# First expert matrix loaded from HBM for each slot instead of copied on the chip from a resident set

## The chip, the cores and the metric

The kernel runs on one core of one Trainium2 chip. The metric is the time of one execution on the device in microseconds (us). Three runs of the kernel before took 895.51, 890.18 and 890.01 us; their median is 890.18 us.

## What is computed

One decoder layer in float32 on x of shape (4, 512, 256): self-attention, cross-attention to a context of 64 rows for each batch, and a mixture of 8 experts with the best 2 for each token, with a layer norm after each. The part that the change touches is the last:

```python
logits = einsum('bsd,ed->bse', x, router_w)          # 8 experts
topk_vals, topk_idx = top_k(softmax(logits), 2)      # for each of 2048 tokens
out = zeros_like(x_flat)                             # 2048 x 256
for eid in range(8):
    w = sum(where(idx == eid, vals, 0), axis=-1)
    h = gelu(x_flat @ w1[eid].T, approximate=False)  # w1[e]: 1024 x 256, 1 MB in float32
    y = h @ w2[eid].T                                # w2[e]: 256 x 1024, 1 MB in float32
    out = out + w[:, None] * y
```

The result is layernorm(x + out).

## The kernel before, in words

The attention stages come first and are not touched. During the second of them and after it SyncE (SP) loads the weights of the experts into `wexp`, one `load_expert(e)` for each expert (lines 462 to 468): two DMAs of 1 MB, w1 and then w2, which wait until the expert before has landed. Experts 0 to 5 are loaded in and just behind the cross-attention, expert 6 when the input of the expert stage has been stored (line 481), and expert 7 between the loads of the meta rows (line 496).

The router decides on the chip which tokens go to which expert. GpSimd (POOL) scatters token numbers and weights into the table `metas` in HBM (line 664, 32 indirect DMAs of 128 rows). VectorE (DVE) makes two plans of 39 entries (`NSLOT` = 39 slots of 128 tokens): `plan[0]` names the expert of each slot, `plan[1]` the row in `metas` where its tokens begin. It signals `s_planned`.

Then the expert stage runs over the 39 slots:

- SP waits for the plan and for all scatters to have landed (lines 484 to 486). For each slot t it reads `plan[1]` into a register and issues a 1 KB DMA from `metas` to `mt` (`load_meta`, lines 488 to 490). The slots form three groups, 0 to 3, 4 to 7 and 8 to 38, written out one behind another, with `load_expert(7)` behind the first group. After this SP has nothing to do until the last sums are stored (line 499).
- POOL gathers the 128 rows of slot t from `x2d` (line 695), three slots ahead of the scatter; later it adds the weighted output of the slot to `acc` (line 703), one slot at a time.
- VectorE and ScalarE (ACT) copy the w1 of the slot's expert from `wexp` to one of two buffers `w1c`, a half each (`copy_w1`, line 361), when slot t-2 has been through its first matmuls (`s_mm1`).
- TensorE (PE) works in order (`tile`, line 1597): `hidden(t+1)` (32 matmuls of w1 and the turned tokens, line 1582), `turn_tile(t+2)` (2 transposes, line 1570), `expert_out(t)` (16 matmuls with w2, line 1593). `hidden(t)` waits for both halves of `w1c` and for the turned tokens.
- ACT copies the turned tokens (line 845) and does the gelu (line 851); DVE weighs the output (line 1209).

Ahead of the loop PE does `turn_tile(0)`, `hidden(0)`, `turn_tile(1)`. All waits of an engine hold up what stands behind them in that engine's list, and SP's list is one such list.

Of the kernel before, what the change touches and what calls it, by code (L numbers as in the profile page):

```python
# [18 lines left out]
ACT = mybir.ActivationFunctionType  # L19
AX = mybir.AxisListType  # L20

P = 128
NB, S, D = 4, 512, 256
# [5 lines left out]
KD = D // P  # L29
NE, FF = 8, 1024  # L30
KF = FF // P
# [14 lines left out]
NSLOT = (2 * T) // P + NE - 1  # L46
# [5 lines left out]
def decoder_layer(nc, x, xT, ctxT, wqT, wkT, wvT, woT, xwq, xbq, xwk, xbk, xwv, xbv, xwo, xbo,  # L52
# [16 lines left out]
    def sb(name, cols, dt, region, rows=P):  # L69

        width = cols * (2 if dt == BF16 else 4)
        at = place.get(region, region)
        place[region] = at + (width + 31) // 32 * 32
        return nc.alloc_sbuf_tensor_at(name, [rows, cols], dt, offset=at)

    def sem(name):
        return ctx.enter_context(nc.semaphore(name))

    def ds(start, n):
        return slice(start, start + n) if isinstance(start, int) else bass.ds(start, n)  # L80
# [39 lines left out]
    plan = [sb(f"plan{i}", NSLOT, I32, R_CONST, 1) for i in range(2)]  # L120
# [69 lines left out]
    rstd = sb("rstd", QT, F32, Y_REG)  # L190
    assert place[Y_REG] <= R_K + 64 * KB

    EW = KD * FF + KF * D
    place[R_Q] = R_Q
    wexp = sb("wexp", NE * EW, F32, R_Q)

    place[R_O] = R_O
    w1c = [sb(f"w1c{i}", KD * FF, F32, R_O) for i in range(2)]
# [77 lines left out]
    s_planned = sem("plan_ready")  # L276
    s_we = sem("expert_weights_loaded")
# [4 lines left out]
    s_xtT = sem("tile_x_copied")  # L282
    s_mm1 = sem("hidden_ready")
    s_h = sem("gelu_ready")
    s_w1c = [sem(f"w1_copied_{k}") for k in range(KD)]
    s_mm2 = sem("expert_out_ready")
    s_yw = sem("weighted_out_ready")
    s_sc = sem("outputs_added")
# [64 lines left out]
    def max2_rows(queue, b):  # L353
        queue.wait_ge(s_m2c, b + 1)
        for hh in range(2):
            for r in range(3):
                queue.dma_start(qst[ROWS + r:ROWS + r + 1, ds(b * H * S + hh * H * S // 2, H * S // 2)]
                             .rearrange("p (a t) -> p a t", t=P),
                             mT2[8 * QT * r:8 * QT * (r + 1), hh * P:(hh + 1) * P]).then_inc(s_m2l, 16)

    def copy_w1(engine, copy, t, j, k):

        e = engine.value_load(plan[0][0:1, ds(t, 1)], min_val=0, max_val=NE - 1)
        engine.wait_ge(s_we, 32 * (e + 1))
        if not (isinstance(t, int) and t < 2):
            engine.wait_ge(s_mm1, t - 1)
        copy(w1c[j % 2][:, k * FF:(k + 1) * FF], wexp[:, ds(e * EW + k * FF, FF)]).then_inc(s_w1c[k], 1)  # L367

    def third_part(engine, b, qk):
        p_v = parts[qk][:, :].rearrange("p (m r t) -> p m r t", m=KD, r=3)  # L370
# [4 lines left out]
    def _(sp):  # L375
# [85 lines left out]

        def load_expert(e):
            if e > 0:
                sp.wait_ge(s_we, 32 * e)
            sp.dma_start(wexp[:, ds(e * EW, KD * FF)].rearrange("p (k f) -> p k f", k=KD),
                         w1T[ds(e, 1)].rearrange("e (k p) f -> p (e k) f", p=P)).then_inc(s_we, 16)
            sp.dma_start(wexp[:, ds(e * EW + KD * FF, KF * D)].rearrange("p (k n) -> p k n", k=KF),
                         w2T[ds(e, 1)].rearrange("e (k p) n -> p (e k) n", p=P)).then_inc(s_we, 16)


        for b in range(NB - 1):
            max2_rows(sp, b + 1)
            sp.wait_ge(s_pv2, QT * (b + 1))
            load_expert(b)
        sp.wait_ge(s_pv2, QT * NB)
        for e in range(NB - 1, NE - 2):
            load_expert(e)
        sp.wait_ge(s_pos, NB)
        sp.wait_ge(s_x2[0], 16 * NB)
        sp.wait_ge(s_x2[1], 16 * NB)  # L480
        load_expert(NE - 2)


        sp.wait_ge(s_planned, 1)
        for i in range(2):
            sp.wait_ge(s_disp[i], 16 * NT)

        def load_meta(t, group):
            row = sp.value_load(plan[1][0:1, ds(t, 1)], min_val=0, max_val=PAD_BLOCK * P)
            sp.dma_start(mt[:, 2 * t:2 * t + 2], metas[ds(row, P), :]).then_inc(s_mt[group], 16)  # L490

        for group, (lo, hi) in enumerate(META_GROUPS):
            for t in range(lo, hi):
                load_meta(t, group)
            if group == 0:
                load_expert(NE - 1)


        sp.wait_ge(s_sc, 16 * NSLOT)
        acc_v, out_v = (a.rearrange("(n p) d -> p n d", p=P) for a in (acc, out))  # L500
        xr_v = xr[:, :].rearrange("p (n d) -> p n d", d=D)
# [224 lines left out]
    def _(act):  # L726
# [116 lines left out]
        def copy_xtT(t, j):  # L843
            act.wait_ge(s_tpx, t + 1)
            act.activation(xtT[j % 2][:, :], ps[:, 6, 0:D], ACT.Copy).then_inc(s_xtT, 1)

        def gelu(t, j):
            act.wait_ge(s_mm1, t + 1)
            if not (isinstance(t, int) and t < 2):
                act.wait_ge(s_mm2, t - 1)  # L850
            act.activation(hidT[j % 2][:, :], bank(2 * (j % 2), 2), ACT.Gelu).then_inc(s_h, 1)  # L851

        def w1_half(t, j):
            copy_w1(act, lambda to, of: act.activation(to, of, ACT.Copy), t, j, 1)  # L854

        act.wait_ge(s_planned, 1)
        w1_half(0, 0)
        w1_half(1, 1)
        copy_xtT(0, 0)
        gelu(0, 0)  # L860
        copy_xtT(1, 1)
        w1_half(2, 2)
        with act.Fori(0, NSLOT // 4) as i:
            for j in range(4):
                gelu(4 * i + j + 1, j + 1)
                copy_xtT(4 * i + j + 2, j + 2)
                w1_half(4 * i + j + 3, j + 3)
        for t in range(NSLOT // 4 * 4, NSLOT):
            if t + 1 < NSLOT:
                gelu(t + 1, t + 1)  # L870
# [10 lines left out]
    def _(dve):  # L881
# [317 lines left out]
        dve.tensor_copy(plan[1][:, :], planf[2][:, :]).then_inc(s_planned, 1)  # L1199


        def w1_half(t, j):
            copy_w1(dve, dve.tensor_copy, t, j, 0)

        def weigh(t):
            dve.wait_ge(s_mm2, t + 1)
            if t >= 2:
                dve.wait_ge(s_sc, 16 * (t - 1))
            dve.tensor_scalar(yw[t % 2][:, :], ps[:, 4 + t % 2, 0:D], slot_meta(t, 1), None, ALU.mult).then_inc(s_yw, 1)  # L1209

        dve.wait_ge(s_planned, 1)
        w1_half(0, 0)
        w1_half(1, 1)
        for group, (lo, hi) in enumerate(META_GROUPS):
            dve.wait_ge(s_mt[group], 16 * (hi - lo))
            for t in range(lo, hi):
                if t + 2 < NSLOT:
                    w1_half(t + 2, t)
                weigh(t)


# [19 lines left out]
    def _(pe):  # L1241
# [323 lines left out]
        def turn_tile(t, j, turn):  # L1565
            pe.wait_ge(s_g[j % 2], 16 * (turn + 1))
            if not (isinstance(t, int) and t == 0):
                pe.wait_ge(s_xtT, t)
            for k in range(KD):
                mm = pe.transpose(ps[:, 6, k * P:(k + 1) * P], xt[j % 2][:, k * P:(k + 1) * P], identf[:, :])  # L1570
            mm.then_inc(s_tpx, 1)

        def hidden(t, j):

            for k in range(KD):
                pe.wait_ge(s_w1c[k], t + 1)
            pe.wait_ge(s_xtT, t + 1)
            if not (isinstance(t, int) and t < 2):
                pe.wait_ge(s_h, t - 1)
            for f in range(KF):  # L1580
                for k in range(KD):
                    mm = pe.matmul(ps[:, 2 * (j % 2) + f // 4, f % 4 * P:(f % 4 + 1) * P],  # L1582
                                   w1c[j % 2][:, k * FF + f * P:k * FF + (f + 1) * P], xtT[j % 2][:, k * P:(k + 1) * P],
                                   start=(k == 0), stop=(k == KD - 1))
            mm.then_inc(s_mm1, 1)

        def expert_out(t, j):
            e = pe.value_load(plan[0][0:1, ds(t, 1)], min_val=0, max_val=NE - 1)
            pe.wait_ge(s_h, t + 1)
            if not (isinstance(t, int) and t < 2):  # L1590
                pe.wait_ge(s_yw, t - 1)
            for f in range(KF):
                mm = pe.matmul(ps[:, 4 + j % 2, 0:D], hidT[j % 2][:, f * P:(f + 1) * P],  # L1593
                               wexp[:, ds(e * EW + KD * FF + f * D, D)], start=(f == 0), stop=(f == KF - 1))
            mm.then_inc(s_mm2, 1)

        def tile(t, j, i):
            last = isinstance(t, int)
            if not (last and t + 1 >= NSLOT):
                hidden(t + 1, j + 1)  # L1600
            if not (last and t + 2 >= NSLOT):
                turn_tile(t + 2, j, 2 * i + j // 2 + 1)
            expert_out(t, j)

        pe.wait_ge(s_planned, 1)
        turn_tile(0, 0, 0)
        hidden(0, 0)
        turn_tile(1, 1, 0)
        for j in range(4):
            tile(j, j, 0)  # L1610
        with pe.Fori(1, NSLOT // 4) as i:
            for j in range(4):
                tile(4 * i + j, j, i)
        for t in range(NSLOT // 4 * 4, NSLOT):
            tile(t, t % 4, t // 4)
# [29 lines left out]
```

## Time and profile before

| what | value |
|---|---|
| median of three runs | 890.18 us (890.01 to 895.51) |
| profiled execution, its own time | 897.14 us |
| span from first to last instruction in it | 895.4 us |
| PE matmuls busy | 688.3 us, 77% |
| DVE / ACT / POOL busy | 377.0 / 322.3 / 218.7 us |
| mean granted TensorE clock | 0.884 of full speed |
| read from HBM / written | 50.45 MB / 21.40 MB |

All times in the rows are those of the one profiled execution, in us from the start of its span. Busy time of an engine is not by itself the bound: what counts in a stretch is which wait ends last there.

### The profile page before, as it was taken

Reading aid. Unit: us, or ns where it says so; the run is one execution under the profiler, and the core shown is the slowest. Engines: PE = TensorE matmul, PEld = TensorE weight load, DVE = VectorE, ACT = ScalarE, POOL = GpSimd, SP = SyncE. Lnnn points to the kernel's source line nnn. Section 1 sums busy time; section 2 is a strip of 40 time slices with the busy share of each in tenths; the row PEclk is TensorE's granted clock in tenths of the full one; section 3 lists DMA queues with packets and bytes.
Section 4 is the critical chain, followed back from the end, with each engine's and each line's share of the span. In section 5 each row is a group of like instructions: output and inputs, shape, how many; then the busy total and the mean of one; then the engine's idle time right before and its main releaser. Section 6 shows DMA issues by size and latency. Waiting matters only on the chain.

```text
span 895.4 us, 13630 instructions
## 1 busy us (share of the span) xinstructions
PE 688.3 (77%) x4099; PEld 451.6 (50%) x4100; DVE 377.0 (42%) x789; ACT 322.3 (36%) x541; POOL 218.7 (24%) x265
## 2 busy tenths in 40 slices
PE   7562365999999986765677862099999999999980
PEld 3231111222222245542213652089999999999970
DVE  2251344988888446664444875001111111111114
ACT  2220133767676643333354212033333333333312
POOL 1021200111111122112111167223333344343322
PEclk9876786999999998886789985589999999999995
DMA  6999993000001431859835815312112112222105
GB/s 193 132 170 168 119 170 39 3 1 1 1 1 52 126 53 38 129 83 134 138 100 191 279 49 142 106 23 37 31 27 35 25 29 35 31 33 32 22 10 187
DMA packets 67346, 71.11 MB, mean 79 GB/s; under 512 B 14548, under 2 KB 60141, under 8 KB 67310
## 3 DMA queue, kind: packets, MB, share of 16 engines
q1 hardware_dynamic: 54574, 58.03, 33.8%
q0 software_dynamic: 8512, 8.44, 6.0%
q10 hardware_dynamic: 4224, 4.19, 1.6%
q8 instruction: 19, 0.31, 0.2%
q14 instruction: 17, 0.14, 0.1%
HBM read 50.45 MB, written 21.40 MB: 80 GB/s over the span
## 4 chain that ended last, share of the span: by engine, by line
PE 65%; DMA 14%; DVE 7%; SPq 4%; POOL 4%; issue 3%; ACT 2%; DVEq 0%; ACTq 0%; POOLq 0%
PE ps L1582 16%; PE ps L1593 15%; PE ps L1303 7%; PE ps L1312 7%; PE ps L1248 6%; DMA scrq<-parts 5%; DMA qst<-mT 5%; POOL metas L664 3%; PE ps L1396 3%; SPq L401 2%; PE ps L1469 2%; PE ps L1462 2%; DMA qst<-scr_q 1%; PE ps L1408 1%; PE ps L1428 1%
## 5 line engine op out<-in xcount | busy, mean ns | idle before, releaser
L898 DVE TENSOR_REDUCE nmx<-ps 128x1 f32<-128x512 f32 x256 | 160.2, 681 | 55.3 <-PE ps L1248 55.3
L745 ACT ACTIVATE probs<-ps 128x512 f32<-128x512 f32 x256 | 133.7, 607 | 94.0 <-PE ps L1303 93.7
L1582 PEld LDWEIGHTS ps<-xtT,w1c 128*128 128x128 f32 x1248 | 148.1, 195 | 4.3 <-DVE w1c L367 1.5
L1582 PE MATMUL ps<-xtT,w1c 128*128 128x128 f32 x1248 | 148.5, 278 | 1.8 <-DVE w1c L367 1.3
L1593 PE MATMUL ps<-wexp,hidT 128*128 x624 | 141.0, 379 | 0.0
L1303 PE MATMUL ps<-qst,kst 99*128 (+1 forms) x256 | 96.0, 395 | 34.9 <-DMA qst<-mT 32.9
L1593 PEld LDWEIGHTS ps<-wexp,hidT 128*128 128x128 f32 x624 | 115.7, 190 | 14.0
L1248 PE MATMUL ps<-kst,qst 96*128 (+1 forms) x256 | 94.1, 393 | 34.9 <-DMA kst<-scrk 17.5
L1209 DVE TENSOR_SCALAR yw<-ps,mt 128x256 f32<-128x256 f32 x39 | 18.9, 484 | 219.9 <-PE ps L1593 219.9
L851 ACT ACTIVATE hidT<-ps 128x1024 f32<-128x1024 f32 x39 | 39.9, 1023 | 195.8 <-PE ps L1582 190.9
L703 POOL DMA_INDIRECT acc<-yw,mt x39 | 68.0, 1742 | 165.8 <-DVE yw L1209 161.4
L1303 PEld LDWEIGHTS ps<-qst,kst 99*128 (+1 forms) x256 | 23.8, 99 | 121.2 <-issue 92.9
L1312 PE MATMUL ps<-probs,vu 128*32 128x512 f32 x512 | 68.2, 605 | 1.9 <-ACT probs L745 1.4
L1248 PEld LDWEIGHTS ps<-kst,qst 96*128 (+1 forms) x256 | 25.4, 100 | 66.9 <-issue 27.9
L808 ACT ACTIVATE probs<-ps 64x512 f32<-64x512 f32 x64 | 35.3, 586 | 42.6 <-PE ps L1462 42.5
L695 POOL DMA_INDIRECT xt<-x2d,mt x39 | 40.7, 1044 | 34.9 <-DMA mt<-metas 12.1
L532 POOL TENSOR_TENSOR m<-nmx,one 128x16 bf16<-128x16 f32 x16 | 3.5, 216 | 181.7 <-PE ps L1248 111.3
L367 DVE COPY w1c<-wexp 128x1024 f32 x39 | 27.2, 697 | 49.0 <-PE ps L1582 31.7
L854 ACT ACTIVATE w1c<-wexp 128x1024 f32 x39 | 41.2, 1058 | 9.3 <-DMA wexp<-in_w2T 9.3
L1570 PE MATMUL ps<-identf,xt 128*128 128x128 f32 x78 | 15.2, 277 | 31.2 <-DMA xt<-x2d,mt 31.2
L1462 PE MATMUL ps<-qst,k2st 99*64 99x512 bf16 x64 | 27.0, 470 | 15.7 <-DMA qst<-mT 10.1
L664 POOL DMA_INDIRECT metas<-meta,slot x32 | 32.2, 1007 | 23.9 <-DVE slot L1148 14.8
(165 smaller groups left out, 695.4 us busy)
## 6 DMA issues: line engine op xcount, KB each, us to landing
wexp<-in_w1T SPq DMA_DIRECT2D x8, 1024.0 KB
wexp<-in_w2T SPq DMA_DIRECT2D x8, 1024.0 KB
qst<-scrq SPq DMA_DIRECT2D x24, 256.0 KB, 9.8
kst<-scrk SPq DMA_DIRECT2D x24, 256.0 KB, 19.7
qst<-scr_q SPq DMA_DIRECT2D x24, 256.0 KB, 8.8
scrq<-parts SPq DMA_DIRECT2D x4, 768.0 KB, 18.6
scrk<-parts SPq DMA_DIRECT2D x4, 768.0 KB, 19.4
scr_q<-parts SPq DMA_DIRECT2D x4, 768.0 KB, 3.4
```

The source lines that it names most:

```text
L664: pool.indirect_dma_start(metas, bass.IndirectOffsetOnAxis(slot[b % 2][:, k * QT + t:k * QT + t + 1], 0), meta[k][:, 2 * (QT * b + t):2 * ...
L695: pool.indirect_dma_start(xt[t % 2][:, :], None, x2d, bass.IndirectOffsetOnAxis(slot_meta(t, 0).bitcast(U32), 0), **checked()).then_inc(s_ ...
L703: pool.indirect_dma_start(acc, bass.IndirectOffsetOnAxis(slot_meta(t, 0).bitcast(U32), 0), yw[t % 2][:, :], None, **checked(), compute_op= ...
L745: act.activation(probs[n % 8][:, :], ps[:, 4 + n % 3, :], ACT.Exp).then_inc(s_exp, 1)
L854: copy_w1(act, lambda to, of: act.activation(to, of, ACT.Copy), t, j, 1)
L898: dve.tensor_reduce(nmx[j % 2][:, k:k + 1], ps[:, slot, :], AX.X, ALU.max, negate=True).then_inc(s_mfree, 1)
L1248: pe.matmul(ps[:, tile_slot(j, k, isinstance(w, int) and w == 0), :], qst[0:ROWS, ds((w * HG + h) * S + qt * P, P)], kst[0:ROWS, ds((w * H ...
L1303: pe.matmul(ps[:, 4 + n % 3, :], kst[:, ds((u * HG + h) * S + kt * P, P)], qst[:, ds((u * HG + h) * S, S)], start=True, stop=True).then_in ...
L1312: mm = pe.matmul(ps[VW * h:VW * (h + 1), 7, :], vu[j % 2][:, (kt * HG + h) * VW:(kt * HG + h + 1) * VW], probs[(kt % 2) * HG + h][:, :], s ...
L1462: pe.matmul(ps[0:SC, 4 + h % 2, :], k2st[0:MROWS, ds((h * NB + b) * SC, SC)], qst[0:MROWS, ds((b * H + h) * S, S)], start=True, stop=True) ...
L1582: mm = pe.matmul(ps[:, 2 * (j % 2) + f // 4, f % 4 * P:(f % 4 + 1) * P], w1c[j % 2][:, k * FF + f * P:k * FF + (f + 1) * P], xtT[j % 2][:, ...
L1593: mm = pe.matmul(ps[:, 4 + j % 2, 0:D], hidT[j % 2][:, f * P:(f + 1) * P], wexp[:, ds(e * EW + KD * FF + f * D, D)], start=(f == 0), stop= ...
```

## The change

`wexp` keeps only the w2 of the experts (8 MB in all). Each `load_expert` is one DMA of 1 MB. The w1 of slot t is loaded by SP from HBM into `w1c[t % 2]`, with the expert's number read from `plan[0]`; the copies of DVE and ACT are gone. Slot 0's load stands behind the wait for the plan and ahead of the wait for the scatters, slot 1's behind the first group of meta loads, and those of slots 2 to 38 behind the last group of meta loads. From slot 2 on each waits until slot t-2 has been through its first matmuls.

```diff
-    EW = KD * FF + KF * D
+    EW = KF * D
...
-    s_w1c = [sem(f"w1_copied_{k}") for k in range(KD)]
+    s_w1c = [sem(f"w1_loaded_{k}") for k in range(2)]
...
-    def copy_w1(engine, copy, t, j, k):
-
-        e = engine.value_load(plan[0][0:1, ds(t, 1)], min_val=0, max_val=NE - 1)
-        engine.wait_ge(s_we, 32 * (e + 1))
-        if not (isinstance(t, int) and t < 2):
-            engine.wait_ge(s_mm1, t - 1)
-        copy(w1c[j % 2][:, k * FF:(k + 1) * FF], wexp[:, ds(e * EW + k * FF, FF)]).then_inc(s_w1c[k], 1)
...
         def load_expert(e):
             if e > 0:
-                sp.wait_ge(s_we, 32 * e)
-            sp.dma_start(wexp[:, ds(e * EW, KD * FF)].rearrange("p (k f) -> p k f", k=KD),
-                         w1T[ds(e, 1)].rearrange("e (k p) f -> p (e k) f", p=P)).then_inc(s_we, 16)
-            sp.dma_start(wexp[:, ds(e * EW + KD * FF, KF * D)].rearrange("p (k n) -> p k n", k=KF),
+                sp.wait_ge(s_we, 16 * e)
+            sp.dma_start(wexp[:, ds(e * EW, KF * D)].rearrange("p (k n) -> p k n", k=KF),
                          w2T[ds(e, 1)].rearrange("e (k p) n -> p (e k) n", p=P)).then_inc(s_we, 16)
...
-        for e in range(NB - 1, NE - 2):
+        for e in range(NB - 1, NE):
             load_expert(e)
...
-        load_expert(NE - 2)
-
+
+        def load_w1(t, j):
+            e = sp.value_load(plan[0][0:1, ds(t, 1)], min_val=0, max_val=NE - 1)
+            if not (isinstance(t, int) and t < 2):
+                sp.wait_ge(s_mm1, t - 1)
+            sp.dma_start(w1c[j % 2][:, :].rearrange("p (k f) -> p k f", k=KD),
+                         w1T[ds(e, 1)].rearrange("e (k p) f -> p (e k) f", p=P)).then_inc(s_w1c[j % 2], 16)
 
         sp.wait_ge(s_planned, 1)
+        load_w1(0, 0)
         for i in range(2):
             sp.wait_ge(s_disp[i], 16 * NT)
...
             if group == 0:
-                load_expert(NE - 1)
-
-
+                load_w1(1, 1)
+
+
+        for t in range(2, NSLOT):
+            load_w1(t, t)
         sp.wait_ge(s_sc, 16 * NSLOT)
...
-        w1_half(0, 0)
-        w1_half(1, 1)
...
-        w1_half(2, 2)
...
-                w1_half(4 * i + j + 3, j + 3)
...
-                if t + 2 < NSLOT:
-                    w1_half(t + 2, t)
...
-        def hidden(t, j):
-
-            for k in range(KD):
-                pe.wait_ge(s_w1c[k], t + 1)
+        def hidden(t, j, turn):
+
+            pe.wait_ge(s_w1c[j % 2], 16 * (turn + 1))
...
-                               wexp[:, ds(e * EW + KD * FF + f * D, D)], start=(f == 0), stop=(f == KF - 1))
+                               wexp[:, ds(e * EW + f * D, D)], start=(f == 0), stop=(f == KF - 1))
...
         pe.wait_ge(s_planned, 1)
+        pe.wait_ge(s_we, 16 * NE)
         turn_tile(0, 0, 0)
-        hidden(0, 0)
+        hidden(0, 0, 0)
```

## Rows read from the trace of the kernel before

**Rows 1.** The page's slices of the span, 40 equal ones: granted TensorE clock in tenths.
```profile
PEclk9876786999999998886789985589999999999995
```

**Rows 2.** Chain that ended last, expert stage: start us, us, what.
```profile
598.52 3.57 PE ps L1582 x32
...
859.34 3.57 PE ps L1582 x32
```

**Rows 3.** Timeline of PE: start us, us, engine, line, operation, tiles, count, idle before.
```profile
583.02 6.54 PE L1582 MATMUL ps<-xtT,w1c 128*128 128x128 f32 x32 [0.56 <-ACT xtT L845]
...
591.04 3.81 PE L1582 MATMUL ps<-xtT,w1c 128*128 128x128 f32 x32 [1.26 <-DVE w1c L367]
...
598.36 3.73 PE L1582 MATMUL ps<-xtT,w1c 128*128 128x128 f32 x32
```

**Rows 4.** Groups by line, 598.3 to 845: busy us, mean ns, idle before.
```profile
L854 ACT ACTIVATE w1c<-wexp 128x1024 f32 x34 | 36.0, 1058 | 0.0
...
L367 DVE COPY w1c<-wexp 128x1024 f32 x34 | 23.7, 697 | 15.2 <-issue 15.2
```

**Rows 5.** Chain that ended last, from the last scatter to the first gather.
```profile
562.26 5.95 DMA metas<-meta,slot
...
572.71 1.68 DMA mt<-metas
...
575.31 6.35 DMA xt<-x2d,mt
```

**Rows 6.** Timeline of SP's queue, 568 to 616 (DMA issues only).
```profile
569.30 3.75 SPq L490 DMA_DIRECT2D mt<-metas  x4
573.09 0.43 SPq L465 DMA_DIRECT2D wexp<-in_w1T  x1
573.57 0.47 SPq L467 DMA_DIRECT2D wexp<-in_w2T  x1
574.79 8.09 SPq L490 DMA_DIRECT2D mt<-metas  x8
...
612.60 1.43 SPq L490 DMA_DIRECT2D mt<-metas  x2
```

**Rows 7.** Timeline of POOL, four of the scatters behind the plan.
```profile
552.33 1.19 POOL L664 DMA_INDIRECT metas<-meta,slot  x1 [0.30 <-issue]
553.83 1.22 POOL L664 DMA_INDIRECT metas<-meta,slot  x1 [0.30 <-issue]
...
556.61 1.56 POOL L664 DMA_INDIRECT metas<-meta,slot  x1 [0.30 <-issue]
558.48 0.95 POOL L664 DMA_INDIRECT metas<-meta,slot  x1 [0.30 <-issue]
```

**Rows 8.** Stretches: engines' busy us (count), granted clock, DMA share, GB/s.
```profile
574.00:575.00 1.00, 0.00 (x0) 0.00 (x0) 0.00 (x0) 0.00 (x0) 0.00 (x0) 0.50 0.88 66
575.00:576.00 1.00, 0.00 (x0) 0.00 (x0) 0.00 (x0) 0.00 (x0) 0.69 (x1) 0.50 0.97 385
576.00:577.00 1.00, 0.00 (x0) 0.00 (x0) 0.00 (x0) 0.00 (x0) 0.69 (x2) 0.50 0.99 410
577.00:578.00 1.00, 0.00 (x0) 0.00 (x0) 0.00 (x0) 0.00 (x0) 0.66 (x1) 0.50 1.01 381
```

**Rows 9.** Stretches in and behind a pause of PE in the cross-attention, same columns.
```profile
430.00:432.00 2.00, 0.34 (x4) 0.00 (x0) 1.92 (x3) 0.00 (x0) 1.44 (x2) 1.00 1.17 118
...
435.00:436.00 1.00, 0.00 (x0) 0.00 (x0) 0.00 (x0) 0.00 (x0) 0.00 (x0) 0.57 0.47 45
```

**Rows 10.** POOL's slot in the steady state, and a scatter's landing in the chain.
```profile
621.58 1.78 POOL L703 DMA_INDIRECT acc<-yw,mt  x1 [4.12 <-DVE yw L1209]
623.66 1.05 POOL L695 DMA_INDIRECT xt<-x2d,mt  x1 [0.30 <-issue]
...
867.65 2.67 DMA acc<-yw,mt
```

More of the change, by code:

```diff
@@ L851, in gelu @@
             act.activation(hidT[j % 2][:, :], bank(2 * (j % 2), 2), ACT.Gelu).then_inc(s_h, 1)
-        def w1_half(t, j):
-            copy_w1(act, lambda to, of: act.activation(to, of, ACT.Copy), t, j, 1)
-        act.wait_ge(s_planned, 1)
-        w1_half(0, 0)
-        w1_half(1, 1)
         copy_xtT(0, 0)
@@ L1199, in _ @@
         dve.tensor_copy(plan[1][:, :], planf[2][:, :]).then_inc(s_planned, 1)
-        def w1_half(t, j):
-            copy_w1(dve, dve.tensor_copy, t, j, 0)
         def weigh(t):
@@ L1211, in _ @@
         dve.wait_ge(s_planned, 1)
-        w1_half(0, 0)
-        w1_half(1, 1)
         for group, (lo, hi) in enumerate(META_GROUPS):
@@ L1599, in tile @@
             if not (last and t + 1 >= NSLOT):
-                hidden(t + 1, j + 1)
+                hidden(t + 1, j + 1, 2 * i + (j + 1) // 2)
             if not (last and t + 2 >= NSLOT):
```

## The prediction

> **What bounds the kernel now.** I read the slices of the page first, then the chain of waits through the expert stage, then each queue's timeline at the start of that stage. The slices show a granted clock near full speed through the last third, with a dip to half just ahead of it [rows 1]. The chain of the last third is TensorE alone: hidden(2) at 598.52 and hidden(38) at 859.34 [rows 2], 36 slots in 260.82 us, so 7.245 us a slot. The copies that the change removes lie beside this: 1.058 us on ScalarE and 0.697 us on VectorE a slot [rows 4], and after slot 2 no row of PE in the chain waits for them. PE's timeline names VectorE's copy at 591.04, for 1.26 us [rows 3], but hidden(1) also needs the copy of its turned tokens, which ScalarE does behind the gelu of slot 0; the w1 of slot 1 was copied long before. So removing the copies is worth 0 us: PE's own matmuls cover them.
>
> What decides is the start of the stage. The last scatter is issued at 562.26 and lands 5.95 us later, at 568.2; the first group of meta rows lands at 574.4; the first gather takes 6.35 us from 575.31 [rows 5]; hidden(0) runs from 583.02, hidden(1) from 591.04, hidden(2) from 598.36 [rows 3]. Meanwhile SP issues one meta load after another: the first four from 569.30, eight more from 574.79 in 8.09 us, the last two from 612.60, ending at 614.03 [rows 6]. Between the issue at 574.79 and that end stand 35 meta loads in 39.24 us, 1.12 us each, of which the DMA issue itself is about a third: reading the plan into a register is the larger part. Today nobody waits for this list, since the third group is wanted only at slot 8. In the changed kernel the w1 of slots 2 to 38 stands behind it.
>
> **The change, part by part.**
>
> Removed copies: 0 us, as above. If their cover went, they would cost or give 1.06 us a slot; it does not, since PE has no idle time in the steady state.
>
> Smaller expert loads ahead of the plan: SP moves 8 MB instead of 14 before the plan. PE, VectorE and ScalarE bound those stretches and no step of the chain there waits for a load of an expert. 0 us; the load of expert 6, 2 MB in the shadow of the scatters, becomes w1 of slot 0, 1 MB, issued a few us later. Three scatters issued beside it took 1.19, 1.22 and 1.56 us instead of 0.95 [rows 7], 1.1 us in all; with half the bytes I keep half: the last scatter lands 0.5 us earlier (bounds: 1.1 earlier, or 0.5 later if the load meets the last ones).
>
> Slot 1's load takes the place of the 2 MB behind the first group. It costs SP one read of the plan more and one DMA issue less, +0.2 us by [rows 6]: today 1.70 us pass from the first of the two big issues to the next meta issue; then 0.77 + 0.4 + 0.77 us, less the 0.04 us between issue and issue today. The first gather has half the bytes ahead of it, so its 6.35 us may fall by 2 us; hidden(0) and hidden(1) start that much earlier, but they are no longer what the stage waits for.
>
> The added wait: hidden(2) needs w1 of slot 2. SP ends its last meta issue at 614.03. Eight issues in 8.09 us at 0.34 us each leave 0.77 us between an issue and the next [rows 6], so this load would be issued at 614.80; with -0.5 and +0.2 it is 614.5. Its own wait, for hidden(0), is long met.
>
> How long 1 MB takes is not shown for one load alone. The pair of 1 MB loads issued at 573.09 moved 0.07, 0.39, 0.41 and 0.38 MB in the four us from 574 [rows 8]; the first 1.05 MB were through at 577.5, 4.4 us after the issue. That is the lower bound. The upper one is 7.2 us, what the whole pair needs at 0.38 MB a us, as if the load had to share its engines for all its length. I take 4.7, near the lower row, since it is the same shape and queue, with 0.3 for the end of the transfer. The Trainium skill's page "DMA: Bandwidth & Descriptors", section Bandwidth, gives 6.15 us of transfer for 1 MB on the path issued from GpSimd; by it the sum would be 1.8 us larger or more, and the 1.05 MB in 3.5 us of [rows 8] speak against it for this queue.
>
> So w1 of slot 2 lands at 619.2 and hidden(2) starts at 619.3 instead of 598.36: **20.9 us** of PE idle in which everything behind it in PE's list, turn_tile(3) and expert_out(1) too, stands still. Slot 3's load is issued one step later (about 1.1 us) and lands by 623, before hidden(3).
>
> The clock: in the cross-attention the granted clock was full in the two us from 430, in which PE had only 0.34 us of work, and fell to half in the us from 435 [rows 9]. So a pause of about 5 us was enough, and one of 20 us cools it too. Hidden(0) at 583.02 ran at half clock, 1.2 of 2.4 GHz, for most of its length and took 6.54 us; a warm one takes 3.73 [rows 3]. Hidden(2) costs **2.8 us** more (bounds: 1.4, the clock back halfway through the same work, and 3.7, all of it cold).
>
> The steady state: SP may issue load t when hidden(t-2) has ended, and hidden(t) starts a slot plus 3.66 us later, 10.9 us. Read, issue and landing take 0.8 + 4.7 = 5.5 us; half of the time is spare. The transfers meet POOL's. A scatter lands 2.67 us from its issue and the next may start then; with gather the list takes 1.78 + 0.30 + 1.05 us of 7.245 [rows 10]. With the whole 2.8 us that 1 MB occupies the engines in front of it, a scatter lands in 5.5 us, still inside the slot. The gather issued at 623.66 is that of slot 7; PE wants it when hidden(6) ends, at 598.52 + 4 x 7.245 + 3.57 = 631.1 [rows 2]. If it took 6.35 us like the first one beside 2 MB [rows 5] it would land at 630.0, with 1.1 us to spare. 0 us a slot, bounds 0 and 1.
>
> Sum: 20.9 + 2.8 = **23.7 us**. Against the profiled execution's own 897.14 us that is 920.8, and a span of 919.1. The median of the runs stands 6.96 us below the profiled time, so 890.18 + 23.7 = **913.9 us**.
>
> **Rivals.**
>
> *SP's list is short.* The stage would then have no stall, and the kernel ends not slower. The place is the list of 39 meta loads; the mechanism, that the issue of a small load costs SP little. It decides where w1 of slot 2 is issued by 593.8 (hidden(2) at its old 598.36, less 4.7), which over some 39 steps from 569.3 asks for 0.63 us a step; the rows show 1.12. The time it gives: the first gather shorter by 2 us and nothing else, 888 us. The Trainium skill says this in "DMA: Bandwidth & Descriptors", section Issuing engines are not separate DMA queues: the sequencer's time to initiate a DMA "is usually small relative to the DMA itself". By that rule the time is this rival's; against it here stands a list that takes 45 us for 39 KB. An execution without the profiler may step faster, but hardly by 44%. Chance 0.06.
>
> *Contention in every slot.* The w1 transfers push the scatters or gathers past PE's need, 1 us a slot over 35 slots on top of the forecast: 949 us. For it: 1 MB for each 7.245 us is 145 GB/s where there were some 30. Against it: the margins of 1.1 us at worst and some 5 us for the loads. Chance 0.05.
>
> *The stall is partly hidden.* The list steps some 20% faster unprofiled and the clock comes back fast: 9 us less from the list and 1.4 from the clock, 13.3 left, 903 us. The runs are 7 us shorter than the profiled execution, which I can't place. Chance 0.12. My forecast: 0.75. The remaining 0.02 is for something unseen.
>
> **How the numbers follow.** Prediction 913.9 us. Low end: list 10% faster (-4.5), scatters earlier by another 0.6, clock 1.4 less: 907; stretched to 905 towards the partly hidden case. High end: landing 7.2 us (+2.5), clock +0.9, and a median that falls where the 895.51 run lies, of which I count two thirds (+3.5): 921. A difference under 1% (8.9 us) is what a measurement of this kernel can hardly tell from none. Faster by over 1%: 0.02; within 1%: 0.05, the first rival; slower by over 1%: 0.93.
>
> **What would show it.** In the profile after: SP's issue of w1 for slot 2 at about 614.5, right behind the last meta load; PE idle from about 596 to 619, put down to the DMA of `w1c`; granted clock 0.50 in that gap and hidden(2) at about 6.5 us; then slots of 7.245 us with no wait of PE for `w1c`, and loads issued at the end of each hidden. It would be wrong if the meta loads step at under 0.7 us, if the w1 loads land in over 10 us, or if PE waits again in the steady state.

## The result and the profile after

The changed kernel took 918.49 us, median of four runs (916.85 to 919.41), beside 890.1 us for the kernel before: ratio 1.031, 95% interval 1.027 to 1.036. Measured a second time beside more runs of the kernel before, it came to 1.0235 (1.0196 to 1.0273), which is 21 us. The forecast of 913.9 us was 23.7 us over 890.18. Medians given below are of all runs; the ratios leave out single runs that took clearly longer than the others of the same kernel (three of ten, 911 to 914 us against 890 to 898, for the kernel with 1.5 MB a slot), so a ratio here can differ from the quotient of two medians.

The profiled execution after has a span of 915.1 us against 895.4, 19.7 us more, though hidden(2) alone is late by more than that. (The profiled execution before, 897.14 us, was longer than each run in the median, and the one after, 916.85 us, is the shortest of its four.) To compare the expert stages I count from the issue of the last scatter, 562.26 before [rows 5]. After, it is at 558.97, the last row of POOL's timeline ahead of the stage:

```profile
558.97 0.96 POOL L662 DMA_INDIRECT metas<-meta,slot  x1 [0.31 <-issue]
```

SP's queue after (DMA issues alone, start and length in us), which answers to [rows 6]:

```profile
566.34 3.66 SPq L486 DMA_DIRECT2D mt<-metas  x4
570.75 0.39 SPq L476 DMA_DIRECT2D w1c<-in_w1T  x1
571.91 38.06 SPq L486 DMA_DIRECT2D mt<-metas  x35
610.76 76.72 SPq L476 DMA_DIRECT2D w1c<-in_w1T  x12
```

The 35 meta loads take 38.06 us, 1.09 us each, and the w1 of slot 2 is issued at 610.76, 0.79 us behind the end of the last of them (571.91 + 38.06 = 609.97). PE's timeline after, to be laid beside [rows 3]:

```profile
577.52 6.18 PE L1564 MATMUL ps<-xtT,w1c 128*128 128x128 f32 x32 [0.57 <-ACT xtT L843]
...
585.18 3.81 PE L1564 MATMUL ps<-xtT,w1c 128*128 128x128 f32 x32 [1.26 <-ACT xtT L843]
...
615.74 5.88 PE L1564 MATMUL ps<-xtT,w1c 128*128 128x128 f32 x32 [23.07 <-DMA w1c<-in_w1T]
...
625.13 3.73 PE L1564 MATMUL ps<-xtT,w1c 128*128 128x128 f32 x32
...
632.37 3.73 PE L1564 MATMUL ps<-xtT,w1c 128*128 128x128 f32 x32
...
878.81 3.73 PE L1564 MATMUL ps<-xtT,w1c 128*128 128x128 f32 x32
```

Three things stand in it. Hidden(2) waited 23.07 us for its matrix. It then took 5.88 us, where a warm one takes 3.73. And from hidden(4) at 632.37 to hidden(38) at 878.81 lie 34 slots of 7.248 us: the steady state is what it was. The groups of waits from 600 us on show the same: one wait of PE's matmuls for `w1c`, and no other.

```profile
PE ps L1564 <- DMA w1c<-in_w1T: 23.1, 1, 23.1
```

The chain of waits names who held that DMA back. It runs through SP's reads of the plan (L485) and meta issues (L486) to the read for slot 2 (L473):

```profile
608.92 0.27 SPq L485
609.22 0.15 SPq L485
609.44 0.05 issue
609.64 0.34 SPq L486
610.02 0.27 SPq L473
...
610.76 4.93 DMA w1c<-in_w1T
615.74 5.88 PE ps L1564 x32
```

The clock in and behind the pause (busy us of PE, PEld, DVE, ACT, POOL, then granted clock, DMA share, GB/s); PE had stopped at 592.67:

```profile
595.00:596.00 1.00, 0.00 (x0) 0.00 (x0) 0.00 (x0) 0.00 (x0) 0.74 (x1) 1.00 0.07 1
596.00:597.00 1.00, 0.00 (x0) 0.00 (x0) 0.00 (x0) 0.00 (x0) 0.95 (x1) 0.58 0.58 57
...
619.00:620.00 1.00, 1.00 (x7) 1.00 (x7) 0.00 (x0) 0.00 (x0) 0.00 (x0) 0.50 0.00 0
620.00:621.00 1.00, 1.00 (x10) 1.00 (x10) 0.00 (x0) 0.00 (x0) 0.00 (x0) 0.98 0.00 0
```

By these rows it fell from full (2.4 GHz) to half (1.2 GHz) 3.5 us into the pause and came back at 620.0, 4.3 us after PE resumed.

From the last scatter's issue to hidden(38) the stage takes 296.92 us before (from 562.26 [rows 5] to 859.18 in PE's timeline) and 319.84 after: **22.9 us more**. This is the change. The early stages, which it hardly touches, differ more from one execution to the next than I had allowed: see the first experiment.

### The profile page after: what moved, and what is told of

It is laid out like the page before. It is cut to its first block, busy times and chain, and to the rows that moved or that the text cites. A ratio compares the mean times of both kernels' runs of the same rounds, so it can differ in the third digit from the quotient of the medians.

```text
span 915.1 us, 13249 instructions
## 1 busy us (share of the span) xinstructions
PE 693.1 (76%) x4099; PEld 454.0 (50%) x4100; DVE 350.1 (38%) x750; ACT 285.5 (31%) x501; POOL 212.3 (23%) x265
## 4 chain that ended last, share of the span: by engine, by line
PE 61%; DMA 14%; SPq 8%; DVE 7%; issue 4%; POOL 3%; ACT 2%; DVEq 0%; ACTq 0%; POOLq 0%
PE ps L1564 15%; PE ps L1575 14%; DMA scrq<-parts 7%; PE ps L1286 7%; PE ps L1295 7%; PE ps L1231 5%; SPq L393 3%; POOL metas L662 3%; PE ps L1379 3%; DMA qst<-mT 3%; SPq L485 2%; PE ps L1452 2%; SPq L486 2%; PE ps L1445 2%; PE ps L1411 1%
## 5 line engine op out<-in xcount | busy, mean ns | idle before, releaser
L701 POOL DMA_INDIRECT acc<-yw,mt x39 | 61.7, 1582 | 197.5 <-DVE yw L1196 192.9
L1553 PE MATMUL ps<-identf,xt 128*128 128x128 f32 x78 | 15.2, 277 | 28.4 <-DMA xt<-x2d,mt 28.4
L1391 PE MATMUL ps<-identf,xr 128*128 128x128 f32 x64 | 14.4, 367 | 22.5 <-DVE xr L991 21.8
L876 DVE SCALAR_TENSOR_TENSOR tmp<-ps,parts 128x1024 f32<-128x1024 f32 x8 | 9.8, 1220 | 56.5 <-ACT parts L730 56.5
## 6 DMA issues: line engine op xcount, KB each, us to landing
scrk<-parts SPq DMA_DIRECT2D x4, 768.0 KB, 18.6
```

What stands on the lines that cost most here:

```text
L701: pool.indirect_dma_start(acc, bass.IndirectOffsetOnAxis(slot_meta(t, 0).bitcast(U32), 0), yw[t % 2][:, :], None, **checked(), compute_op= ...
```

## Experiments

For each kernel I give the ratio to the kernel before on its chip, and from its trace the stage's length, last scatter's issue to the start of hidden(38). The stage's length is the finer measure, since it leaves the early stages out. Two profiles of the kernel before have 296.92 and 295.65 us, two of the changed kernel 319.84 and 318.78. So two profiles of one kernel differ by 1.1 to 1.3 us, and a difference of 1 or 2 us says little by itself. It says more when it is taken apart. Where PE has no stall and 1 MB or less is loaded for each slot, the stage is the start of hidden(0), plus the length of hidden(0), plus 269.6 us (269.61 to 269.62 in five profiles: the kernel before twice, and three kernels below). Where hidden(2) stalls, it is the start of hidden(2), plus its length, plus 257.1 us (257.08 to 257.19 in five profiles). Starts are counted from the last scatter's issue. So the spread lies in those two terms, the start and the cold length of the first or the stalled hidden.

**The kernel before again** (no edit).

> The kernel before, run again against itself. Both theories: ratio 1.00. Its profile is for the stretch ahead of the expert stage: if that stretch differs from one profiled execution to the next by several us (last scatter issued at 562.3 in the first profile of this kernel, at 559.0 in that of the changed one), the part of the measured 28.4 us that the expert stage does not hold (22.8 us there) is the spread of the early stages, not the change.

Ratio 1.0015 (0.998 to 1.005). The last scatter was issued at 556.53, 5.7 us earlier than in the first profile of the same code. Over all 13 profiles of the study that time runs from 553.55 to 568.26, without regard to the edits. So a comparison of two single spans says little here about differences under some 15 us.

**The changed kernel again** (no edit).

> The changed kernel again, beside this chip's own runs of the kernel before. If the expert stage alone makes the difference (22.8 us there), the ratio is about 1.026 and the first comparison's 1.031 was partly the early stages' spread; if the change costs something ahead of the expert stage too, the ratio stays at 1.031 and the last scatter is issued later than in the kernel before.

Ratio 1.0235. Last scatter at 561.00, between the 556.53 and 562.26 of the kernel before; stage 318.78 us. The means of the two pairs, 319.3 and 296.3, differ by 23.0 us, 2.6% of 890, inside the interval of this comparison and just under that of the first one. The excess of the first, 28.4 against 23 us, is not found in any stage of the trace (from hidden(38) to the end both profiles take 36.2 to 36.3 us); that it is the early stages' spread is likely, not shown.

**One load moved ahead.**

```diff
             for t in range(lo, hi):
                 load_meta(t, group)
+                if t == 11:
+                    load_w1(2, 2)
...
-        for t in range(2, NSLOT):
+        for t in range(3, NSLOT):
             load_w1(t, t)
```

> The changed kernel with the load of slot 2's first matrix moved from behind the 39 meta loads to behind the twelfth. List theory (SP's own time for the meta loads holds the w1 loads back): hidden(2) no longer waits; the list ends 1.1 us later, so that slot 3's matrix lands 1.1 us later than slot 2's did, and hidden(3) stalls until about 57.9 us behind the last scatter's issue instead of running from 66.3. Gain against the changed kernel 6 us (8.4 less the cold clock that hidden(3) now pays): ratio to the kernel before about 1.024. Rival (the loads themselves or the contention are slow): time unchanged at 1.031.

Ratio 1.026 (1.021 to 1.031), which can't tell this kernel from the changed one. The stage takes 317.19 us: 2.1 us gained on the mean of the changed kernel's two, not 6. The stall did move to slot 3, as PE's timeline shows:

```profile
586.26 3.73 PE L1566 MATMUL ps<-xtT,w1c 128*128 128x128 f32 x32
...
614.34 6.56 PE L1566 MATMUL ps<-xtT,w1c 128*128 128x128 f32 x32 [20.66 <-DMA w1c<-in_w1T]
```

And SP's queue shows why so little came of it:

```profile
566.19 8.04 SPq L486 DMA_DIRECT2D mt<-metas  x8
577.64 0.39 SPq L476 DMA_DIRECT2D w1c<-in_w1T  x1
578.80 29.62 SPq L486 DMA_DIRECT2D mt<-metas  x27
609.50 77.16 SPq L476 DMA_DIRECT2D w1c<-in_w1T  x12
```

The eight meta loads end at 574.23, the load of slot 2 waits for hidden(0), which ends at 577.5, and the 27 meta loads behind it wait too: 3.4 us from the end of one issue to the start of the next where 0.77 would do. I had the place in the list too early by about three meta loads. Slot 3's matrix is issued 55.95 us behind the last scatter, 4.2 us later than slot 2's was in the changed kernel (51.79), where I had expected 1.1: that is 3.1 us. Hidden(3) also ran colder than hidden(2) had (6.56 against 5.88 us): 0.7 us. The expectation of 6.1 us, less 3.1 and 0.7, leaves 2.3 us, near what was measured. So the theory holds with these two counted, and it shows how a wait put in a list delays everything behind it.

**The loads between the meta loads.**

```diff
+        at = {11: 2, 17: 3, 23: 4, 29: 5, 35: 6}
         for group, (lo, hi) in enumerate(META_GROUPS):
             for t in range(lo, hi):
                 load_meta(t, group)
+                if t in at:
+                    load_w1(at[t], at[t])
...
-        for t in range(2, NSLOT):
+        for t in range(7, NSLOT):
             load_w1(t, t)
```

> The changed kernel with the w1 loads of slots 2 to 6 put between the meta loads (behind slot 11's, 17's, 23's, 29's and 35's). List theory: no PE wait for w1c at all, steady state 7.245 us a slot, and the first gather 2.2 us shorter than before: 888 us, ratio 0.9975. Rival (contention of 1 MB a slot): slots longer than 7.245 us, ratio above 1.01.

Ratio 0.996 (0.9935 to 0.9986), stage 293.73 us: 25.6 us less than the changed kernel and 2.6 less than the kernel before. Of the 2.6, 1.6 us are an earlier hidden(0) (18.63 us behind the last scatter, against 20.76 and 19.75), and 0.9 its shorter cold length (5.49 us, against 6.54 and 6.28), which varies from profile to profile. Nothing but the order in SP's list differs from the changed kernel, so the 25.6 us are that order's. PE's timeline has no wait for `w1c` any more (the 1.26 us ahead of hidden(1) are the copy of its tokens, as before):

```profile
585.08 3.81 PE L1567 MATMUL ps<-xtT,w1c 128*128 128x128 f32 x32 [1.26 <-ACT xtT L846]
...
592.40 3.73 PE L1567 MATMUL ps<-xtT,w1c 128*128 128x128 f32 x32
...
599.64 3.73 PE L1567 MATMUL ps<-xtT,w1c 128*128 128x128 f32 x32
```

**The meta loads twice.**

```diff
+    mt_again = sb("mt_again", 2 * NSLOT, F32, R_O)
...
+        for t in range(8, NSLOT):
+            row = sp.value_load(plan[1][0:1, ds(t, 1)], min_val=0, max_val=PAD_BLOCK * P)
+            sp.dma_start(mt_again[:, 2 * t:2 * t + 2], metas[ds(row, P), :]).then_inc(s_again, 16)
...
+        sp.wait_ge(s_again, 16 * (NSLOT - 8))
```

> The changed kernel with the meta loads of slots 8 to 38 issued a second time, into a spare tile that nobody reads, ahead of the w1 loads: 31 KB more of transfer. List theory: 31 steps of 1.10 us more of SP, PE's wait for slot 2's matrix grows from 23 to 57 us, 952 us. Rival (bytes or transfers count, not SP's steps): under 1 us more.

954.18 us (two runs), ratio 1.067 (1.061 to 1.073), stage 354.0 us: 34.7 more than the changed kernel for 31 steps, 1.12 us a step. The second list on SP, the load behind it in the chain that ended last, and PE's wait:

```profile
613.00 33.98 SPq L497 DMA_DIRECT2D mt_again<-metas  x31
...
647.74 4.79 DMA w1c<-in_w1T
...
652.57 5.87 PE L1570 MATMUL ps<-xtT,w1c 128*128 128x128 f32 x32 [57.59 <-DMA w1c<-in_w1T]
```

31 KB more of transfer moved the end by 35 us. The w1 of slot 2 is issued right behind the last step and lands in 4.8 us, as in the changed kernel (4.9), so nothing had piled up in the DMA queue: the steps on SP are what costs. Which part of a step costs most, the read of the plan or the DMA issue, no run separates.

**The loads on ScalarE's queue.**

```diff
-        load_w1(0, 0)
...
-                load_w1(1, 1)
...
-        for t in range(2, NSLOT):
-            load_w1(t, t)
...
+        def load_w1(t, j):
+            e = act.value_load(plan[0][0:1, ds(t, 1)], min_val=0, max_val=NE - 1)
...
+            act.dma_start(w1c[j % 2][:, :].rearrange("p (k f) -> p k f", k=KD),
+                          w1T[ds(e, 1)].rearrange("e (k p) f -> p (e k) f", p=P)).then_inc(s_w1c[j % 2], 16)
...
+        load_w1(0, 0)
+        load_w1(1, 1)
         copy_xtT(0, 0)
...
+        load_w1(2, 2)
...
                 copy_xtT(4 * i + j + 2, j + 2)
+                load_w1(4 * i + j + 3, j + 3)
```

> The changed kernel with all w1 loads issued by ScalarE, where the copies stood, and none by SP. List theory: SP's meta list no longer holds anything back, no wait of PE for w1c, as with the loads put between the meta loads: ratio 0.996 to 0.998. Rival (it was the order in one DMA queue or the transfers): a wait remains.

Ratio 0.998 (0.994 to 1.001), stage 293.71 us, as with the loads between the meta loads (293.73), though SP's list of 39 meta loads stands unbroken:

```profile
575.95 43.39 SPq L478 DMA_DIRECT2D mt<-metas  x39
```

No row of PE waits for `w1c` in this trace. A list of 43 us harms nobody when nothing urgent is behind it. The stall is due neither to the transfers nor to the DMA engines, which carry the same bytes here.

**PE kept busy in the pause**, with 190 and then with 223 transposes ahead of hidden(2).

```diff
         for j in range(4):
+            if j == 1:
+                for n in range(223):
+                    pe.transpose(ps[:, 7, n % 4 * P:(n % 4 + 1) * P], identf[:, :], identf[:, :])
             tile(j, j, 0)
```

> The changed kernel with 190 transposes of the identity, into a bank nobody reads, between expert_out(0) and hidden(2), 21.2 us at full clock, inside the 23.1 us of PE's wait. Theory: the wait stays, the clock stays at 1.00, hidden(2) takes 3.7 instead of 5.9 us, 2.2 us less than the changed kernel. Rival (the pause does not matter for the clock): no change.

> The changed kernel with 223 transposes of the identity instead of 190 in PE's wait, 24.5 us at full clock, which leaves no pause ahead of hidden(2). With 190 a pause of 3.3 us was left and hidden(2) still ran cold, 5.3 us. Theory: clock 1.00 throughout, hidden(2) 3.7 us; against the changed kernel 1.7 to 2.2 us less, minus what the transposes run over the landing (up to 1 us): ratio about 1.022. Rival: hidden(2) is slow for another reason than the clock (its matrix is still landing, say): still above 5 us.

With 190 the expectation failed: PE stopped for 3.29 us, and that was enough. Hidden(2) took 5.33 us and the stage 320.14; the ratio, 1.020 (1.015 to 1.026), can't tell 2 us. Hidden(2) also started later, 57.7 us behind the last scatter against 56.8 and 56.3, since SP's list issued its matrix later in this profile (52.7 us, against 51.8 and 51.5). With 223 the pause is gone and hidden(2) is warm; its row follows that of the transposes:

```profile
586.80 24.51 PE L1595 MATMUL ps<-identf 128*128 128x128 f32 x223
611.15 3.74 PE L1564 MATMUL ps<-xtT,w1c 128*128 128x128 f32 x32
```

The stage took 317.43 us, 1.9 less than the changed kernel's mean. The ratio of 1.026 (1.020 to 1.031), where about 1.022 was expected, does not show it, and 1.9 us is little above the spread between two profiles. The trace shows the gain all the same: hidden(2) takes 3.74 us instead of 5.88 and 5.39, and what follows it takes the same 257.1 us in all of them. So the cold clock costs 1.65 to 2.14 us, and the rival (a matrix that is still landing) falls. In the run with 190 the clock was 1.00 up to 623 and fell in the us from 623, with PE stopped at 620.82:

```profile
623.00:624.00 1.00, 0.00 (x0) 0.00 (x0) 0.00 (x0) 0.00 (x0) 0.00 (x0) 0.93 1.04 410
624.00:626.00 2.00, 1.88 (x9) 1.89 (x10) 0.00 (x0) 0.00 (x0) 0.00 (x0) 0.50 0.95 385
```

**More bytes a slot.** The loads between the meta loads, and from slot 4 on a further load into a spare buffer: the whole matrix again, or half of it (`w1x[t % 2][:, 0:FF]` from `w1T[ds(e, 1), 0:P]`). The edit for the whole matrix:

```diff
+            if t >= 4:
+                if t >= 6:
+                    sp.wait_ge(s_more[t % 2], 16 * (t // 2 - 2))
+                sp.dma_start(w1x[t % 2][:, :].rearrange("p (k f) -> p k f", k=KD),
+                             w1T[ds(e, 1)].rearrange("e (k p) f -> p (e k) f", p=P)).then_inc(s_more[t % 2], 16)
```

> The kernel with the w1 loads between the meta loads, and from slot 4 on each matrix loaded a second time into a spare buffer that nobody reads: 2 MB a slot. My margins (load 5.5 of 10.9 us, gather's landing 1.1 us to spare at worst) say: slots stay at 7.245 us, within 2 us of that kernel. Rival (contention is close by): each slot grows, 1 us a slot is 35 us.

> The kernel with the w1 loads between the meta loads and from slot 4 on 0.5 MB more a slot into a spare buffer: 1.5 MB a slot. With 1 MB the slots took 7.245 us and gathers landed in 5.0 us, with 2 MB 8.39 us and 6.0 us. If the limit is the landing of the scatter beside the loads, a serial chain on POOL of scatter, landing, scatter, that chain was 8.4 us at 2 MB and is under 7.25 at 1 MB; at 1.5 MB it lies near 7.25, slots take 7.25 to 7.8 us, ratio 0.996 to 1.015. If the limit is the gather's landing, whose margin was 1.1 us above 6.35 us, nothing changes: 0.996.

2 MB a slot: ratio 1.040 (1.034 to 1.045), stage 333.09 us. The expectation (within 2 us) was wrong by 37: slots took 8.39 us. With 1.5 MB: ratio 0.999 (0.995 to 1.004), stage 296.39 us, inside what was expected. But the average of 7.33 us a slot misleads, for the 3.0 us that are lost are not spread. Hidden(6), (7), (8) and (9) start 8.1, 7.5, 8.0 and 8.3 us after the one before; from hidden(10) at 654.92 to hidden(38) at 857.94 a slot takes 7.25 us again:

```profile
623.91 3.81 PE L1577 MATMUL ps<-xtT,w1c 128*128 128x128 f32 x32 [0.67 <-DMA w1c<-in_w1T]
...
647.68 3.73 PE L1577 MATMUL ps<-xtT,w1c 128*128 128x128 f32 x32
654.92 3.73 PE L1577 MATMUL ps<-xtT,w1c 128*128 128x128 f32 x32
```

At the start of these four slots SP works off what its meta list held back: w1 loads go out at 618.7, 623.3 and 627.9, 4.6 us apart, where later they are 7.2 apart, and three scatters on POOL, at 617.42, 626.78 and 633.94, are held by the one before. So 1.5 MB a slot goes by without loss once the slots are even; that the crowd of loads behind the list made the loss is likely, not shown.

In 2 MB's trace POOL's scatters follow each other at 8.40 us (702.34, 710.74), though the output is weighed at 706.89, each held until the one before has landed. In the kernel with the loads between the meta loads, where 1 MB a slot goes by, they follow the weighing, 7.24 us apart. First the rows with 2 MB, then those with 1 MB:

```profile
706.41 0.48 DVE L1209 TENSOR_SCALAR yw<-ps,mt 128x256 f32<-128x256 f32 x1 [7.50 <-PE ps L1588]
...
710.12 0.44 PE L1566 MATMUL ps<-identf,xt 128*128 128x128 f32 x2 [0.17 <-DMA xt<-x2d,mt]
...
710.74 1.58 POOL L714 DMA_INDIRECT acc<-yw,mt  x1 [5.47 <-PE ps L1566]
```

```profile
702.56 1.58 POOL L704 DMA_INDIRECT acc<-yw,mt  x1 [4.31 <-DVE yw L1199]
...
709.80 1.59 POOL L704 DMA_INDIRECT acc<-yw,mt  x1 [4.31 <-DVE yw L1199]
```

The releaser that the first fence names for POOL is inferred and cannot be right, since the scatter waits in the code only for its weighed output and for the scatter before it; the groups of waits of the same trace put 105.7 us in 20 waits down to the scatter before:

```profile
POOL acc L714 <- DMA acc<-yw,mt: 105.7, 20, 6.3
```

PE feels it through the gather, which stands behind the scatter in POOL's list and landed in 6.0 us (median). The scatters landed in 7.6 us (median, 6.4 to 8.4), where they took 3.8 with 1 MB a slot and 4.0 in the second profile of the kernel before. So the steady state is covered at 1 MB a slot, in this trace at 1.5 MB too but for four slots, and at 2 MB it is not.

Bytes a slot are not the whole of it. At the same 1 MB the gathers land in 5.0 us (median) with the loads between the meta loads and in 2.8 us, as in the kernel before, with the loads on ScalarE's queue. In the first SP issues the load 0.5 us behind the start of POOL's gather (704.99 against 704.44), in the second ScalarE does so 1.4 us behind it (707.33 against 705.96). That this order makes the difference is my reading of two traces; no run varied it alone.

**The version that beats both.** The loads between the meta loads, with slot 1's matrix loaded ahead of the wait for the scatters and slot 0's meta row as a group of its own.

```diff
-META_GROUPS = ((0, 4), (4, 8), (8, NSLOT))
+META_GROUPS = ((0, 1), (1, 4), (4, 8), (8, NSLOT))
...
         load_w1(0, 0)
+        load_w1(1, 1)
...
-            if group == 0:
-                load_w1(1, 1)
```

> The kernel with the w1 loads between the meta loads, with two edits more that the traces point to: slot 1's matrix is loaded right behind slot 0's, ahead of the wait for the scatters, so that nothing stands beside the first gather; and slot 0's meta row is a group of its own, so that the first gather waits for one step of SP's list and not for four. List theory: hidden(0) starts 3.3 us earlier by the three steps and 1 us by the shorter gather, at 14.3 us behind the last scatter's issue instead of 18.6: 887 us, ratio 0.991. Rival (the scatter's landing or the gather's fixed time hold the start): 0.996 as before.

884.20 us, ratio **0.9895** (0.986 to 0.993), stage 290.63 us. The last scatter was issued at 559.33 and hidden(0) started 14.50 us later (14.3 expected, 18.6 without these edits). By the interval it is faster than the kernel before, by about 1%. The first gather and hidden(0):

```profile
569.55 1.05 POOL L695 DMA_INDIRECT xt<-x2d,mt  x1 [9.27 <-DMA mt<-metas]
...
573.83 6.51 PE L1566 MATMUL ps<-xtT,w1c 128*128 128x128 f32 x32 [0.56 <-ACT xtT L845]
```

Three steps of the list were in front of the first gather too, in every kernel so far. Of the 4.1 us that hidden(0) gains, 1.1 are the gather's (2.92 against 3.98 us in the chains) and 3.3 the list's, less 0.3 for a last scatter that landed later. The stage keeps 3.1, since hidden(0) ran cold for longer (6.51 against 5.49 us).

## Why the prediction was right

- **The list on SP.** Forecast: w1 of slot 2 issued at 614.5, which is 52.7 us behind the last scatter's issue, since the forecast put that 0.5 us earlier than [rows 5] (52.2 without this). Measured 51.8, and 51.5 in the second profile of the changed kernel. The step is 1.09 us (1.12 forecast). That this list sets the time is shown by three runs: steps doubled, loads moved between, loads moved off. What a step is made of was read too boldly: the forecast called the read of the plan the larger part, and the chain after has 0.34 us of DMA issue, 0.27 us of read, 0.15 us of register work and the rest in short pieces and gaps.
- **The landing.** 4.7 forecast; 4.98 from issue to PE's start, 4.80 in the second profile. The Trainium skill's 6.15 us for 1 MB ("DMA: Bandwidth & Descriptors", Bandwidth) are for loads issued from GpSimd; this one, issued by SP, took less.
- **The stall.** Hidden(2) forecast at 57.0 to 57.5 us behind the last scatter's issue, measured 56.8 and 56.3. Against the first profile of the kernel before [rows 3] that is 20.7 us later, between the two second profiles 21.5; 20.9 forecast.
- **The clock.** 2.8 us forecast; 2.15 and 1.66 measured (5.88 and 5.39 us against 3.73), and the run that kept PE busy removed it. This is the sum's one clear excess. I took hidden(0)'s return to full clock for hidden(2)'s; it varies from run to run (hidden(0) took 5.49 to 6.54 us over the profiles). The pause of "about 5 us" that the forecast read as enough was too long as well: 3.5 us did in the profile after, and 3.3 us in the run with 190 transposes.
- **Removed copies.** 0 forecast, nothing found: with them gone and no stall (loads between the meta loads) the slots are still 7.245 us. The reading of the 1.26 us ahead of hidden(1) was right too: the second profile of the kernel before puts them down to ScalarE's copy of the tokens, and they are there without any copy of w1.
- **The first gather.** Up to 2 us, without effect on the end: hidden(0) starts 18.55 and 18.03 us behind the last scatter instead of 20.76 [rows 3, 5] and 19.75, and the stall swallows it. In the kernels without a stall it is most of what makes them faster than the kernel before; the rest is how long hidden(0) stays cold. The gather itself took 6.35 us beside 2 MB [rows 5], 3.98 beside 1 MB, 2.92 beside none (the chains of the kernel with the loads between the meta loads and of the best one). That fewer bytes beside it are the cause fits these three, and no run varied them alone.
- **The scatters in front.** 0.5 us earlier forecast; not to be measured under a spread of 15 us in that time. Two were slow after (1.19 and 1.23 us), three before [rows 7].
- **The steady state.** 0 forecast and found, but for a reason only half right. I put a scatter at 5.5 us beside 1 MB, and it landed in 3.8; the load lengthens the gather instead, from 2.8 to 5.0 us. I trusted the gather's 6.35 us as the worst [rows 5, 10], and beside 2 MB it is the chain of scatters that runs at 8.4 us a slot and PE with it. The rival of contention was nearer than I argued: twice the bytes bring it about, and 1.5 times touch it in four slots.
- **The rival of a short list**, by which the time would have been 888 us, fell: the step did not go under 1.09 us. So the rule of the Trainium skill ("DMA: Bandwidth & Descriptors", Issuing engines are not separate DMA queues) does not carry to this list: a step of SP, 1.09 us, is less than the 1.7 us in which a meta load lands, but landings overlap and steps do not, and 31 steps more cost 35 us. (The rival's 593.8 goes by the chain's 598.52 and not by the 598.36 that it names; nothing rests on this.)
- **The sum.** 23.7 forecast, 23.0 in the traces (21.1 for the stall and 1.9 for the clock, as means of two pairs), 21 and 28 by the two comparisons of runs. So the mechanism and its size were right; that the first comparison's 918.5 us stayed under the range's end of 921 owes something to the allowances made there for other terms, since the spread between comparisons was not among them except for the median's 3.5 us.

## What to carry to other kernels

Count an in-order queue that issues DMAs as an engine with a time for each step, the read of an address register included, and put what is wanted first at its head: here the same loads in another order were worth 26 us. Before a wait goes into such a list, price what stands behind it. And when a transfer is added under a steady state that looks idle, look at the serial chains that wait for small transfers to land, since here they set the pace at 250 GB/s of loads, where single stretches reached 410.

## What the hardware showed that was not expected

- A step of SP with a value read from SBUF cost 1.09 to 1.12 us, of which 0.34 us is the DMA issue, 0.27 the read of the plan and 0.15 the register work behind it; the remaining 0.33 us are short pieces and gaps.
- A pause of PE of 3.3 us was enough for the clock to be at half when it resumed (0.93 in the us around the fall, 0.50 behind it), and it came back 4.3 us after PE resumed in the profile after.
- An indirect accumulating scatter of 128 KB landed in 2.67 us at the end of the stage [rows 10], in 3.8 us (median) with 1 MB of loads a slot, and held up the next for some 8.4 us, start to start, with 2 MB. 2.1 MB in 8.4 us is 250 GB/s of loads, well under the 410 GB/s of single stretches of 1 us.
- The last scatter, behind stages that the edits hardly touch, was issued anywhere within 15 us over 13 profiled executions.
